# Second layer: left and right sides from one set of products, split once and moved to their partitions by five transfers

## The reference, cut to what matters

```
xn = layernorm(x)
left, right = xn @ compare_left, xn @ compare_right         # 256 x 64 each
comparison = left @ right.T / sqrt(256)                     # 512 x 512 a batch
mask = comparison > threshold
attn = mask * softmax(comparison + gate_bias) @ xn
xr, xk = mu * xn + (1 - mu) * xn_shifted_by_one_row         # two mixes
ffn = sigmoid(xr @ W_r.T) * (square(relu(xk @ W_k.T)) @ W_v.T)
x = x + attn + ffn
```

## Time and profile before

| | us |
|---|---|
| median of 3 runs (lowest, highest) | 1032.87 (1032.01, 1033.13) |
| the profiled execution's own time | 1033.06 |
| its span in the trace | 1031.3 |
| TensorE busy, of the span | 986.5 (96%) |
| VectorE, ScalarE, GpSimd busy | 840.2, 758.7, 768.8 |
| second layer's six full bodies (n = 0 to 5) | 123.32, or 20.55 each |
| bodies 6 and 7 | 24.84 |

### The profile page before, as it was taken

How to read it: one execution, slowest core, us unless ns; L and a number is a source line. 1 busy time by engine, 2 the same in 40 slices (tenths; PEclk the granted TensorE clock), 3 DMA queues, 4 the chain that set the end, 5 groups by cost and what they waited for, 6 DMA issues and landing times.

```text
span 1031.3 us, 23734 instructions
## 1 busy us (share of the span) xinstructions
PE 986.5 (96%) x8004; PEld 677.4 (66%) x8004; DVE 840.2 (81%) x2272; ACT 758.7 (74%) x2014; POOL 768.8 (75%) x941
## 2 busy tenths in 40 slices
PE   5889999999999999999999999999999998999998
PEld 4556655666666666666666666666666665777776
DVE  7998888888879888878778778777778757998875
ACT  5978887666676677676766677676776666999994
POOL 4776667868777787878787878787878546878884
PEclk9999999999999999999999999999999999999999
DMA  8733444243433333333334333433333100000101
GB/s 272 239 109 108 140 125 144 88 128 108 124 120 90 107 109 93 93 113 94 97 94 126 95 96 108 117 93 93 93 98 93 48 1 1 22 22 22 42 22 42
DMA packets 99704, 98.71 MB, mean 96 GB/s; under 512 B 13312, under 2 KB 95360, under 8 KB 98944
## 3 DMA queue, kind: packets, MB, share of 16 engines
q1 hardware_dynamic: 99584, 97.19, 31.1%
HBM read 56.25 MB, written 40.90 MB: 94 GB/s over the span
## 4 chain that ended last, share of the span: by engine, by line
PE 67%; DVE 14%; ACT 8%; issue 4%; POOL 4%; DMA 2%; POOLq 0%; SPq 0%; ACTq 0%; DVEq 0%
PE bank L1649 22%; PE bank L1746 12%; PE bank L1732 11%; PE bank L1763 7%; PE bank L1720 6%; PE bank L1721 5%; POOL arena L628 2%; ACT arena L869 2%; PE bank L1942 2%; DVE arena L1362 2%; PE bank L1884 1%; DVE arena L1519 1%; DVE arena L1378 1%; POOL arena L600 1%; DVE arena L1340 1%
## 5 line engine op out<-in xcount | busy, mean ns | idle before, releaser
L628 POOL TENSOR_SCALAR arena<-arena,rc 128x128 f32<-128x128 f32 (+3 forms) x512 | 279.0, 563 | 182.8 <-DVE rc L1371 181.9
L869 ACT ACTIVATE arena<-arena,nm 128x256 f32<-128x256 f32 (+3 forms) x512 | 284.4, 556 | 113.9 <-DVE nm L1362 109.3
L1362 DVE CUSTOM_DVE_ANT_0 arena<-bank,mask_rows 128x256 f32<-128x256 f32 (+3 forms) x512 | 233.7, 484 | 85.9 <-PE bank L1721 80.7
L1732 PE MATMUL bank<-ident,arena 128*128 128x128 f32 x1280 | 212.1, 278 | 16.5 <-DVE arena L1378 8.8
L1732 PEld LDWEIGHTS bank<-ident,arena 128*128 128x128 f32 x1280 | 149.8, 141 | 76.5 <-DVE arena L1378 33.5
L1721 PE MATMUL bank<-arena 128*128 128x256 f16 (+3 forms) x512 | 152.9, 299 | 0.0
L1746 PE MATMUL bank<-arena 128*64 128x512 f32 (+3 forms) x1024 | 152.0, 439 | 0.0
L1720 PE MATMUL bank<-arena 128*128 128x256 f16 (+3 forms) x512 | 139.9, 300 | 1.6 <-DMA arena<-scr 1.6
L1746 PEld LDWEIGHTS bank<-arena 128*64 128x64 f32 x1024 | 67.8, 136 | 94.8 <-issue 69.8
L1378 DVE COPY arena<-bank 128x512 f32<-128x512 f32 (+3 forms) x256 | 124.8, 488 | 3.9 <-PE bank L1732 3.5
L877 ACT ACTIVATE arena<-bank 128x512 f32<-128x512 f32 (+3 forms) x256 | 108.9, 425 | 14.4 <-PE bank L1732 13.8
(11 more groups left out here) (183 smaller groups left out, 2202.0 us busy)
## 6 DMA issues: line engine op xcount, KB each, us to landing
arena<-scr SPq DMA_DIRECT2D x320, 128.0 KB, 2.7
scr<-arena SPq DMA_DIRECT2D x256, 128.0 KB, 1.7
arena<-in_weights SPq DMA_DIRECT2D x5, 1024.0 KB, 7.6
x_sb<-in_x SPq DMA_DIRECT2D x8, 512.0 KB, 9.1
out<-x_sb SPq DMA_DIRECT2D x16, 256.0 KB, 2.2
xscr<-arena SPq DMA_DIRECT2D x12, 256.0 KB, 3.1
xsh<-xscr SPq DMA_DIRECT2D x6, 256.0 KB, 3.3
xsl<-xscr SPq DMA_DIRECT2D x6, 256.0 KB, 3.6
```

The costliest lines, as they stand in the source:

```text
L628: last = pool.tensor_scalar(pr[slot][:, OFF[i]:OFF[i + 1]], pr[slot][:, OFF[i]:OFF[i + 1]], rc[:, slot, i:i + 1], 1.0, ALU.mult, ALU.mult)
L869: act.activation(pr[slot][:, OFF[i]:OFF[i + 1]], pr[slot][:, OFF[i]:OFF[i + 1]], ACT.Exp, scale=-1.0, bias=nm[:, slot, i:i + 1], accum_out ...
L1362: dve.tensor_tensor_reduce(pr[slot][:, OFF[i]:OFF[i + 1]], s_tile[i], mask_rows[:, SQ - P * (i + 1):SQ], -1.0, -MASKED, ALU.add, ALU.min, ...
L1732: last = pe.transpose(banks[5 + h][:, (i - j) * P:(i - j + 1) * P], pr[2 * par + h][:, OFF[i] + j * P:OFF[i] + (j + 1) * P], ident[:])
```

## The change

One set of six matmuls takes the place of two. Its weights are the middle 128 columns of the same array, left beside right, so that one bank holds left on partitions 0 to 63 and right on 64 to 127. ScalarE makes one high part of it, `side_h`, and VectorE one low part, `side_l`, in a corner of the weight array `wh` that the second layer no longer uses. Five transfers on SyncE's queue bring the halves to `ls3`, `rh3` and `rl3`; the lower half of `rl3` is zero. The bank is bank 0 (bank 2 for batch 0), so `pt3(n+1,0)`, which writes bank 0, now waits for `side_low`. `compare` waits for the transfers.

The order changes too: `sides` moves ahead of the two `av3` and two `key` of its body, `side_high` and `side_low` move forward on their engines, `rows_high` moves from ScalarE to VectorE, between `gate_value(n,1)` and `gated(n+1,2)`, and in the prologue some steps change places.

```diff
+            def move_sides(n):
+                if absent3(n):
+                    return
+                after(sp, lrh_done, made(1, n))
+                for dst, src in ((ls3[0:L], side_h[0:L]), (rh3[0:L], side_h[L:P]), (rh3[L:P], side_h[L:P])):
+                    sp.dma_start(dst, src).then_inc(lr_moved, 16)
+                after(sp, lrl_done, made(1, n))
+                for dst, src in ((ls3[L:P], side_l[0:L]), (rl3[0:L], side_l[L:P])):
+                    sp.dma_start(dst, src).then_inc(lr_moved, 16)
+            move_sides(0)
+            move_sides(1)
             for b in range(NB):
+                move_sides(b + 2)
...
-            def side_high(n, s):
-                after(act, lr_mm, made(2, n, s))
-                after(act, c_mm, made(4, n - 1, 3))
-                act.activation((ls3, rh3)[s], banks[2 + s][:], ACT.Copy).then_inc(lrh_done, 1)
+            def side_high(n):
+                after(act, lr_mm, made(1, n))
+                after(act, lr_moved, 80 * n)
+                act.activation(side_h, banks[0 if n else 2][:], ACT.Copy).then_inc(lrh_done, 1)
...
                 exp3(n + 1, 3, 1 - u)
+                side_high(n + 2)
                 key_relu(n + 1, 0)
-                rows_high(n + 2, u)
                 key_square(n + 1, 0)
                 key_high(n + 1, 0)
-                side_high(n + 2, 0)
                 key_relu(n + 1, 1)
-                side_high(n + 2, 1)
...
+            def rows_high(n, par):
+                after(dve, xn3_done, made(NT, n, NT - 1))
+                after(dve, av3_mm, made(4, n - 2, 3))
+                dve.tensor_copy(xn3h[par], xn3[n % 2]).then_inc(xn3h_done, 1)
+            def side_low(n):
+                after(dve, lrh_done, made(1, n))
+                dve.tensor_tensor(side_l, banks[0 if n else 2][:], side_h, ALU.subtract).then_inc(lrl_done, 1)
...
                 gate_value(n, 1, u)
+                rows_high(n + 2, u)
                 gated(n + 1, 2, 1 - u)
                 gated(n + 1, 3, 1 - u)
+                if n > -2:
+                    side_low(n + 2)
                 mix_all(n + 2, 0)
                 mix_all(n + 2, 1)
                 final(n, 0, u)
                 final(n, 1, u)
                 mix_all(n + 2, 2)
-                side_low(n + 2, 0)
-                side_low(n + 2, 1)
                 pt3_low(n + 1, 0)
                 pt3_low(n + 1, 1)
...
             mix_all(0, 0)
             mix_all(0, 1)
-            side_low(0, 0)
-            side_low(0, 1)
+            side_low(0)
+            mix_all(0, 2)
+            rows_high(0, 0)
             top(0, 0, 0)
-            mix_all(0, 2)
...
-                    a, z = lr_h[:, k, s, :], lr_l[:, k, s, :]
-                    pairs += [(a, xt3h[:, k, :]), (a, xt3l[:, k, :]), (z, xt3h[:, k, :])]
-                product(banks[2 + s][:], pairs, lr_mm)
+                    pairs += [(lr_hf[:, k], xt3h[:, k, :]), (lr_hf[:, k], xt3l[:, k, :]), (lr_lf[:, k], xt3h[:, k, :])]
+                product(banks[0 if n else 2][:], pairs, lr_mm)
...
-                after(pe, lrl_done, made(2, n, 1))
+                after(pe, lr_moved, 80 * (n + 1))
...
+                if j == 0 and not absent3(n + 1):
+                    after(pe, lrl_done, made(1, n + 1))
...
                 compare(n + 1, 2, (xt3l_done, 2, n + 2, 0), (pm3_done, 4, n + 1, 0))
                 compare(n + 1, 3, (xt3l_done, 2, n + 2, 1), (pm3_done, 4, n + 1, 1))
+                sides(n + 2, (pt3l_done, 4, n, 2))
                 av3(n, 2, u)
                 key(n + 1, 0, (er_done, 2, n + 1, 0))
...
                 key(n + 1, 1, (y3a_done, 2, n, 1))
-                sides(n + 2, 0, (pm3_done, 4, n + 1, 2), (xt3l_done, 2, n + 2, 0))
-                sides(n + 2, 1, (pm3_done, 4, n + 1, 3), (xt3l_done, 2, n + 2, 1))
...
-            sides(0, 0, (xt3l_done, 2, 0, 0))
-            sides(0, 1, (xt3l_done, 2, 0, 1))
+            sides(0, (xt3l_done, 2, 0, 0))
             attended(NB - 1, 0, (4, 5, 6, 7), wo)
-            attended(NB - 1, 1, (0, 1), pj)
-            compare(0, 0, (lrl_done, 2, 0, 0))
-            compare(0, 1, (lrl_done, 2, 0, 1))
-            attended(NB - 1, 1, (2, 3, 4, 5, 6, 7), pj)
+            attended(NB - 1, 1, (0, 1, 2, 3), pj)
+            compare(0, 0, (lrl_done, 1, 0, 0))
+            compare(0, 1, (xt3l_done, 2, 0, 1))
+            attended(NB - 1, 1, (4, 5, 6, 7), pj)
```

More of the change, by code:

```diff
@@ L213, in build @@
         kk = carve(KT * SQ).rearrange("p (k s) -> p k s", k=KT)
+        side_h = wh[:, C_QK:C_QK + SQ]
+        side_l = wh[:, C_QK + SQ:C_QK + 2 * SQ]
         st3 = sb("st3", [P, NT, 6], f32)
@@ L316, in build @@
         lrl_done = sem("lrl_done")
+        lr_moved = sem("lr_moved")
+        rl3_zero = sem("rl3_zero")
         mixt_done = sem("mixt_done")
@@ L921, in _ @@
                 ring(n)
[L923 to L929, removed]
             def xt_high(n, k):
@@ L935, in xt_high @@
                 after(act, tr3_mm, made(2, n, k))
-                after(act, lr_mm, made(2, n - 1, 1))
+                after(act, lr_mm, made(1, n - 1))
                 act.activation(xt3h[:, k, :], banks[2 + k][:], ACT.Copy).then_inc(xt3h_done, 1)
@@ L1476, in xt_low3 @@
                 dve.tensor_tensor(xt3l[:, k, :], banks[2 + k][:], xt3h[:, k, :], ALU.subtract).then_inc(xt3l_done, 1)
-            def side_low(n, s):
+            def rows_high(n, par):
                 if absent3(n):
                     return
[L1482 to L1486, removed]
+                after(dve, xn3_done, made(NT, n, NT - 1))
+                after(dve, av3_mm, made(4, n - 2, 3))
+                dve.tensor_copy(xn3h[par], xn3[n % 2]).then_inc(xn3h_done, 1)
+            def side_low(n):
+                if absent3(n):
+                    return
+                after(dve, lrh_done, made(1, n))
+                dve.tensor_tensor(side_l, banks[0 if n else 2][:], side_h, ALU.subtract).then_inc(lrl_done, 1)
             def top(n, p, par):
@@ L1546, in _ @@
             dve.memset(xf3[:, :, 0:1], 0.0).then_inc(xf3_zero, 1)
+            dve.memset(rl3[L:P], 0.0).then_inc(rl3_zero, 1)
             def body3(n, u):
@@ L1856, in turn, with sides @@
                 last.then_inc(tr3_mm, 1)
-            def sides(n, s, *users):
+            lr_hf = wh[:, C_LR:C_WR].rearrange("p (k c) -> p k c", k=KT)[:, :, L:3 * L]
+            lr_lf = wl[:, C_LR:C_WR].rearrange("p (k c) -> p k c", k=KT)[:, :, L:3 * L]
+            def sides(n, *users):
                 if absent3(n):
@@ L1863, in sides @@
                 bank_free(users)
+                if n == 1:
+                    pe.wait_ge(x1_done, 2 * NB)
                 pairs = []
                 for k in range(KT):
-                    a, z = lr_h[:, k, s, :], lr_l[:, k, s, :]
-                    pairs += [(a, xt3h[:, k, :]), (a, xt3l[:, k, :]), (z, xt3h[:, k, :])]
-                product(banks[2 + s][:], pairs, lr_mm)
+                    pairs += [(lr_hf[:, k], xt3h[:, k, :]), (lr_hf[:, k], xt3l[:, k, :]), (lr_lf[:, k], xt3h[:, k, :])]
+                product(banks[0 if n else 2][:], pairs, lr_mm)
             def compare(n, i, *users):
@@ L1873, in compare @@
                     return
-                after(pe, lrl_done, made(2, n, 1))
+                after(pe, lr_moved, 80 * (n + 1))
+                if n == 0:
+                    pe.wait_ge(rl3_zero, 1)
                 bank_free(users)
@@ L1953, in body3 @@
             def body3(n, u):
[L1955 to L1958, removed]
+                turn(n + 2, 0, (pm3_done, 4, n + 1, 0))
+                turn(n + 2, 1, (pm3_done, 4, n + 1, 1))
                 value(n, 1, (er_done, 2, n, 1))
@@ L1974, in body3 @@
                 receptance(n + 1, 1, (kr_done, 2, n + 1, 1))
-                compare(n + 2, 0, (lrl_done, 2, n + 2, 0))
-                compare(n + 2, 1, (lrl_done, 2, n + 2, 1))
+                compare(n + 2, 0, (pm3_done, 4, n + 1, 2))
+                compare(n + 2, 1, (pm3_done, 4, n + 1, 3))
                 av3(n + 1, 0, 1 - u)
```

## The result

| | before | after |
|---|---|---|
| median of 4 runs (lowest, highest), us | 1032.86 (1032.01, 1033.13) | 1049.59 (1048.03, 1050.66) |
| the profiled execution's own time | 1033.06 | 1048.91 |
| its span | 1031.3 | 1047.1 |

The ratio is 1.0157 with a 95% interval of 1.0143 to 1.0171: the change makes the kernel 1.6% slower. The forecast was 1043.6 us, in a range of 1036 to 1050. The median lies 0.4 us inside that range, and two of the four executions (1050.27 and 1050.66) lie above it.

A forecast was written before the change was run, and what follows sets the result against it. TensorE, busy 122.17 of 123.32 us in bodies 0 to 5, was taken as the bound. Terms -2.9, +12.5 and +1.1 gave +10.7 us on 1033.06, 1043.8, with the median at 1043.6 us; range 1036 to 1050.

The forecast's parts named there:

- The step that decides: `rows_high` on VectorE, ahead of the gates, waits for `av3(n,3)` until 9.79 of the body; all behind it waits too.
- the first hole: TensorE stands 1.7 us ahead of `pt3(n+1,0)` in each body, until `side_low` frees its bank.
- the second: TensorE stands 2.1 us ahead of `av3(n+1,0)` in each body, released by VectorE's `pt3_low`.
- The third mix: Last mix behind `final` on VectorE: 1.08 us within the 4.50 taken for two mixes, `final` and third mix.
- rival E: TensorE's clock: should one body run at 1.2 GHz, its 14.5 us in the loop would double, 1058 us; chance 0.03.
- The Newton steps: VectorE, between `top` and `gated(n+2,0)` in bodies 1 and 2: 0.5 us late in each, +1.1 together.
- The transfers: Five a batch on SyncE: hidden by VectorE's lateness; without that cover 0.4 to 1.3 us a body.
- Prologue and body -1: Before body 0, where nothing waits for an `av3`: `av3(0,0)` comes 2.8 to 3.2 us earlier, taken as -2.9.
- the string: VectorE's work from `rows_high` to `pt3_low`, late in bodies 0 to 5: +2.08 us a body, +12.5 us.
- B: VectorE absorbs the delay and TensorE's saving comes out whole, -10.4 us and the 0.48 hole: 1022 to 1020; chance 0.07.
- C: Only the wait of `pt3(n+1,0)` binds: about nothing in the bodies, body -1 -2.9, 1030 us; chance 0.06.
- D: Transfers come late, compare starts at 17.5, body grows by another 0.7: 1048 us, or 1054; chance 0.08.

The follow-up runs named there:

- Experiment 1: The change with `rows_high` put back on ScalarE, behind `key_relu(n+1,0)`: 1030.35 us, ratio 0.9971 to the kernel before.
- experiment 2: The change with `xn3h` in three buffers, so `rows_high`, still on VectorE, waits for the `av3` of the batch before last: 1029.37 us, ratio 0.9959.
- Experiment 3: The kernel before with one edit, `rows_high` on VectorE between `gate_value(n,1)` and `gated(n+1,2)`: 1052.05 us, ratio 1.0183.
- experiment 9: The change plus eight matmuls on constant data ahead of `av3(n+1,0)` in bodies 0 to 5: 1046.43 us, ratio 1.0126 to the kernel before.
- experiment 6: The change plus eight matmuls on constant data ahead of `pt3(n+1,0)` in bodies 0 to 5: 1051.81 us, ratio 1.0183 to the kernel before.
- experiment 7: The change with three `xn3h` buffers and VectorE reordered: `final` ahead of the mixes, `pt3_low` and `top` behind two, third mix last: 1028.46 us, ratio 0.9956.
- experiment 11: The reordered kernel with three `xn3h` buffers, plus four 64 KB transfers on SyncE ahead of the low half's two: 1049.93 us, ratio 1.015.
- experiment 5: The change with `rows_high` moved behind the gates and `side_low` on VectorE, its wait for `av3(n,3)` kept: 1042.59 us, ratio 1.0098.

## Why the prediction was right, point by point

**The step that decides** was right. `rows_high` was to start at 9.79 of the body, and did at 891.01 - 881.16 = 9.85. The idle time was put at some 3.5 us (3.63 measured), the first hole at 1.7 (1.80), the second at 2.1 (1.99), the start of the mixes at 12.50 (893.66 - 881.16 = 12.50). Experiment 1 takes the wait off VectorE, experiment 2 takes it away altogether, and they turn +1.6% into -0.3% and -0.4%. Experiment 3 gives it to the kernel before, which becomes 1.8% slower. That this wait is the cause is shown.

**The number** was less good than the mechanism. The executions are 4.4 to 7.1 us above 1043.6, and the terms below miss in both directions. The range took its upper end for the mixes from +1.0 us a body, though the sentence ahead of it has +1.4, and had nothing for the clock. Without the 3.3 us of the clock the median would lie near 1046; with one more such body it would be outside. That it is inside is in part luck.

**The third mix** was mis-sized. The term "two mixes, `final`, third mix", taken as 4.50 us, measured 898.63 - 893.66 = 4.97. The pair and `final` took 3.40 (3.34 expected), the third mix 1.57 where 1.08 had been read in body 1. A third mix of that length was not new: in body 0 of the kernel before it took 1.64 us, but behind a pair of 1.41, so that the three came to no more than 4.56. Now a long pair and a long third mix fall in the same body, in all six. GpSimd's timeline shows what the third mix met:

```profile
897.00 1.16 POOL L722 TENSOR_TENSOR arena<-arena 128x512 f16<-128x512 f32 x1 [0.42 <-ACT arena L1029]
```

This is `key_low(n+1,1)`, from 897.00 to 898.16. The mix, queued at 897.06, ended at 898.71, 0.55 us later. The Trainium skill's rule in "SBUF — State Buffer", section "SBUF: two separate sides", had been set beside the sum with "some 0.4 us" a body and 2.4 us in all; the trace agrees, with 4.97 - 4.50 = 0.47. From the end of `av3(n,3)` at 890.74 to the start of `av3(n+1,0)` at 899.36 it is 8.62 us where 8.15 were forecast, the rest of the body 14.39 where 14.48 were. That gives the 23.01 measured, and bodies 0 to 5 cost 6 x 2.46 = 14.8 us where 12.5 were forecast.

**The clock** was rival E, with a chance of 0.03 and a price of a whole body. It came in two bodies of the profiled execution, for a small part of each. TensorE's timeline and windows around it:

```profile
945.39 2.62 PE L1965 MATMUL bank<-arena 128*128 128x256 f16 x12 [1.97 <-DVE arena L1524]
```
```profile
945.39:947.80 2.41, 2.41 (x12) 1.79 (x13) 2.31 (x7) 0.77 (x3) 1.33 (x2) 0.53 0.02 7
947.80:950.56 2.76, 2.76 (x22) 2.61 (x22) 2.07 (x7) 2.71 (x7) 0.00 (x0) 0.79 0.00 0
```

The granted clock in the first window is 0.53, close to the lower level of 1.2 GHz, and twelve matmuls take 2.62 us instead of 1.48. The low stretch reaches into the second window, whose mean is 0.79; from 950.56 to the end of the body it is 1.00, which is 2.4 GHz. Price 1.67 us a body, 3.3 in all. That it comes from the idle time of the second hole is shown by experiment 9: with that hole filled no body is above 23.05. My argument against it, that body -1 of the kernel before ran at 1.00 with the same busy share, was wrong twice. The window of body -1 in the earlier trace rows begins at 862.60, 1.30 us ahead of `turn(1)`; from turn to turn TensorE was busy for 17.26 of 19.24 us, or 90% and not 84%. And experiments 6 and 9 show that the share over a body does not decide. Why the clock fell in two bodies and not in all six, whose holes are the same, stays open.

**The Newton steps** were mis-sized the other way. The term was +1.1 us and measured nothing: in body 1 they took 925.20 - 924.04 = 1.2 us instead of 2.5, and the gate behind them waited 0.66 us for the exponential.

**The transfers** were hidden in bodies 0 to 5, as forecast, but with less room than the earlier trace rows promised. Issuing one takes SyncE some 0.59 us and not 0.37; landing is 2.0 us from issue (1.9 to 2.7). In body -1, where no copy waits for an `av3`, they were not hidden: compare waited 0.42 us for one.

**Prologue and body -1** were mis-sized: -2.9 us forecast, and body 0 began 1.98 us earlier than before (881.16 against the 880.2 expected). Of the missing 0.9 us, 0.38 were there already at `turn(0)` (845.65 against 845.27), ahead of most of what was changed; that start lies between 845.0 and 847.4 in the profiles of all the kernels. The forecast also had no term for what TensorE still waits for in body -1, `side_low` ahead of `pt3(0,0)` and a transfer ahead of compare:

```profile
872.07 1.06 PE L1948 MATMUL bank<-ident,arena 128*128 128x128 f32 x8 [0.84 <-DVE wh L1499]
...
875.48 1.04 PE L1664 MATMUL bank<-arena 128*128 128x512 f16 x4 [0.42 <-DMA arena<-wh]
```

The sum of the profiled execution, by its windows: -2.0 up to body 0, +14.8 for the string, +3.3 for the clock, -0.3 in bodies 6 and 7, 15.8 in all, which is 1047.1 - 1031.3. Forecast were -2.9, +12.5, 0, 0 and +1.1. Of the other executions of the changed kernel one is 0.9 us shorter than the profiled one and two are 1.4 and 1.8 us longer; their mean clocks are 0.997, 0.995 and 0.997, so the clock alone doesn't order them.

**Rivals.** B, TensorE's saving whole, needs the wait to go; with it gone, experiments 2 and 7 still have only 3.6 and 4.6 us of the 10.4. By their traces the rest went to long mixes beside GpSimd in experiment 2, to turns that wait behind the statistics and Newton steps in experiment 7, where a body without them takes 19.4 us instead of 20.5, and in both to a body -1 partly at the lower clock (19.2 us where the change has 18.0). No run separates these shares. C did not occur: both holes were there. D did not occur, and experiment 11 shows what it would have cost.

## What to carry to other kernels

Moving an instruction from one engine's queue to another moves its waits too: look up what each of them waits for and when that is over by the new order, and put everything queued behind it on that schedule. Here the copy's wait for a buffer left a whole engine idle for 3.6 us in each body, and its gates 3.1 us late, while a third buffer of 2 KB a partition made the same change a gain. And when a string on VectorE is shifted, read GpSimd's timeline beside it: which operation it meets decides whether a mix takes 0.7 or 2.6 us.

## What the runs showed of the hardware

- A VectorE mix, which has two SBUF inputs, was held until a GpSimd operation that reads SBUF had ended. The mix of 0.74 us alone took 1.65 when `key_low` was running, and a pair took 1.41, 1.91, 3.29 or 3.59 us depending on what it met. The last mix ended 0.54 or 0.55 us behind the end of the GpSimd operation each time: 898.71 and 898.16 in the change, 894.89 and 894.35 in experiment 2, 896.16 and 895.61 in experiment 5. As the earlier trace rows show, long mixes were in the kernel before as well.
- TensorE's clock fell to its lower level behind a hole of 2.0 us, in two of six bodies with such a hole, in which TensorE was busy for 19.2 of 23.0 us at the full clock. It did so too behind a single hole of 2.1 to 2.4 us a body (experiment 5) and behind one of 1.66 us (body -1 of experiments 1, 2, 6 and 7), and cost 1.67 us a body. Useless matmuls in the hole made the kernel 3 us faster; in another hole of the same body they did not help (experiment 6).
- SyncE needs 0.59 us to issue a transfer of 64 KB from SBUF to SBUF, more than for a store of 256 KB (0.37).
